# Attention preparation of a gated cross-attention and expert layer: split around the first scores, V times Wo formed turned

## The reference, cut to what matters

```
x1  = x + tanh(g_xattn) * attention(layernorm(x), ctx)
out = x1 + tanh(g_ffn)  * experts(layernorm(x1))

attention: q = xn Wq^T + bq;  k = ctx Wk^T + bk;  v = ctx Wv^T + bv
           softmax(q k^T / sqrt(512), masked) v Wo^T + bo
experts:   8 experts, each batch's expert takes its 512 best tokens; w1, exact gelu, w2
```

## Time and profile before

| | before |
|---|---|
| median of 3 runs (lowest, highest) | 1584.35 us (1581.07, 1585.58) |
| profiled execution, its own time | 1584.71 us |
| its span in the profile | 1583.0 us |
| mean granted TensorE clock | 0.981 |
| TensorE busy, matmuls and weight loads | 1504.1 us (95%), 1215.4 us (77%) |
| VectorE, ScalarE, GpSimd busy | 1015.0, 749.4, 573.8 us |
| DMA moved | 163.71 MB, mean 103 GB/s |

### The profile page before, as it was taken

One profiled execution on the slowest core, in us unless ns is written; L12 is line 12 of the kernel. 1 busy time (PEld: TensorE's weight loads), 2 busy tenths in 40 slices (PEclk: granted clock), 3 DMA queues, 4 the chain that ended last, 5 costly groups with the idle time before them and its releaser, 6 DMA issues.

```text
span 1583.0 us, 22317 instructions
## 1 busy us (share of the span) xinstructions
PE 1504.1 (95%) x7153; PEld 1215.4 (77%) x7153; DVE 1015.0 (64%) x1704; ACT 749.4 (47%) x1399; POOL 573.8 (36%) x541
## 2 busy tenths in 40 slices
PE   6887588999999999999999999999999999999996
PEld 6444367788788888888888888888888888888885
DVE  1378777556866766576766667576667665766542
ACT  1775133345544545454444454455445454554432
POOL 1265622453444234432444135404442344323311
PEclk9998699999999999999999999999999999999998
DMA  6075522462333442334323434243334423442133
GB/s 230 23 271 195 165 72 80 114 173 80 80 107 92 89 111 83 107 81 108 95 92 81 95 93 121 61 108 86 107 94 87 115 80 107 81 107 80 40 79 68
DMA packets 101479, 163.71 MB, mean 103 GB/s; under 512 B 7418, under 2 KB 45318, under 8 KB 101365
## 3 DMA queue, kind: packets, MB, share of 16 engines
q1 hardware_dynamic: 86965, 128.66, 26.1%
q0 software_dynamic: 14400, 33.56, 11.5%
HBM read 128.64 MB, written 33.55 MB: 102 GB/s over the span
## 4 chain that ended last, share of the span: by engine, by line
PE 85%; DVE 7%; ACT 3%; issue 2%; POOL 1%; DMA 1%; POOLq 0%; SPq 0%; ACTq 0%; DVEq 0%
PE bank L1289 41%; PE bank L1175 33%; PE bank L1149 3%; PE bank L1444 1%; PE bank L544 1%; PE bank L562 1%; DVE w2hl L1134 1%; PE bank L392 1%; DVE count L816 1%; DVE st L781 1%; DVE onehot L1330 1%; DVE atleast L863 1%; DMA ctx_raw<-in_ctx 0%; PE bank L414 0%; ACT xT L612 0%
## 5 line engine op out<-in xcount | busy, mean ns | idle before, releaser
L1289 PE MATMUL bank<-w2hl,hh 128*128 128x512 f32 x2048 | 637.6, 393 | 0.0
L1175 PE MATMUL bank<-xo,whl 128*128 128x512 f32 x2352 | 544.4, 390 | 3.8 <-DVE mix L1239 2.8
L1175 PEld LDWEIGHTS bank<-xo,whl 128*128 128x128 f32 x2352 | 442.1, 188 | 98.5 <-DVE mix L1239 3.7
L1289 PEld LDWEIGHTS bank<-w2hl,hh 128*128 128x128 f32 x2048 | 381.6, 188 | 76.2
L1289 PE MATMUL bank<-w2hl,hid_low 128*128 128x512 f32 x1024 | 399.6, 390 | 0.0
L1289 PEld LDWEIGHTS bank<-w2hl,hid_low 128*128 128x128 f32 x1024 | 192.9, 188 | 40.5
L1394 POOL DMA_INDIRECT layer_out<-y,slot_row x64 | 102.5, 1601 | 302.0 <-ACT y L1309 287.2
L1134 DVE TENSOR_TENSOR w2hl<-raw,w2hl 128x512 fp32r<-128x512 f32 x226 | 160.7, 732 | 54.3 <-ACT w2hl L1129 45.8
L1103 POOL TENSOR_TENSOR whl<-raw,whl 128x512 fp32r<-128x512 f32 x56 | 82.2, 1468 | 260.2 <-ACT whl L1069 260.2
L1129 ACT ACTIVATE w2hl<-raw 128x512 fp32r<-128x512 f32 x228 | 136.5, 624 | 59.9 <-DMA raw<-in_L_ffn_w 41.0
L1108 POOL TENSOR_TENSOR whl<-wsum,whl 128x512 fp32r<-128x512 f32 x56 | 75.0, 1340 | 183.4 <-ACT whl L1090 183.4
(11 more groups left out here) (221 smaller groups left out, 1808.3 us busy)
## 6 DMA issues: line engine op xcount, KB each, us to landing
raw<-in_L_ffn_w SPq DMA_DIRECT2D x228, 256.0 KB, 2.7
raw<-in_L_ffn_w SPq DMA_DIRECT2D x72, 512.0 KB, 4.9
x_s<-in_x SPq DMA_DIRECT2D x8, 1024.0 KB, 6.9
layer_out<-x SPq DMA_DIRECT2D x8, 1024.0 KB, 9.0
xn_rows<-xn SPq DMA_DIRECT2D x8, 1024.0 KB, 4.7
raw_k<-in_L_xattn_Wk SPq DMA_DIRECT2D x1, 1024.0 KB, 5.3
raw_q<-in_L_xattn_Wq SPq DMA_DIRECT2D x1, 1024.0 KB, 11.6
raw_v<-in_L_xattn_Wv SPq DMA_DIRECT2D x1, 1024.0 KB, 13.6
```

Of the source, the lines that this page charges most:

```text
L1175: last = pe.matmul(bk[:, :], whl[:, p % 2, part, 2 * w + k, :], xo[:, xpart, x, k, :], start=(not adds and k == 0 and part == HIGH and xpa ...
L1289: last = pe.matmul(Y_BANKS[c][:, :], high if hpart == HIGH else low[:, c * P:(c + 1) * P], w2hl[:, f % 4, part, :], start=(s == 0 and hpar ...
```

## The change

The list of steps is cut behind `mean`. TensorE, ScalarE and VectorE run the first part, then the attention's iteration 0 (the scores and exponentials of quad 0), and the second part at the head of iteration 1. The turns of Wv 1 and 2, which stood between `cb` and `mean`, are now in the second part; `turn_v` 0 stays in the first.

For the first three quads VectorE takes mean and variance of x by bn_stats and bn_aggr (`lead_stats_dve`), right after its copies of `turn_v` 0, `turn_o` 1 and `turn_o` 3; ScalarE's two passes begin with quad 3.

The product of V and Wo is formed turned: `voT` (two steps, Wo stationary, the 154 columns of both batches' values moving) comes first, VectorE adds bo as a column and multiplies by the gate in one operation, and `vo` is voT turned back. bo is loaded as four rows of 128 with the other biases instead of 77 copies of 512.

Wv, Wo and their turned forms lie in a place of their own (that of `xp` and `hid1`, used later), so that the attention's tiles can be written while they are in use.

```diff
+        outward = ExitStack()
+        with outward:
+            raw_v, raw_o, wvT, woT = (outward.enter_context(nc.sbuf_tensor(n, [P, KD, D], F32))
+                                      for n in ("raw_v", "raw_o", "wvT", "woT"))
         xp = overlay("xp", [P, B, 2, KD, CAP], F32R)
...
             with projections:
-                raw_k, raw_q, raw_v, raw_o, wkT, wvT, woT = (
-                    first(n, [P, KD, D], F32, projections)
-                    for n in ("raw_k", "raw_q", "raw_v", "raw_o", "wkT", "wvT", "woT"))
+                raw_k, raw_q, wkT = (first(n, [P, KD, D], F32, projections) for n in ("raw_k", "raw_q", "wkT"))
             xT = first("xT", [P, 2, KD, Q * P], F32)
...
         add("cb", 0, "act", ("kT", 1))
+        add("mean", 0, "dve", ("qk", 1))
+        SCORES_STEPS = len(steps)
         add("turn_v", 1, "dve")
         add("turn_v", 2, "act")
-        add("mean", 0, "dve", ("qk", 1))
         add("turn_v", 3, "act")
...
             add("turn_o", k, by_turns[k % 2])
+        for h in range(2):
+            add("voT", h, "dve", ("turn_o", KD - 1))
         for b in range(B):
-            add("vo", b, "dve", ("turn_o", KD - 1))
-        for b in range(B):
-            add("voT", b, "act", ("vo", b))
-        add("vg", 0, "dve", ("voT", B - 1))
+            add("vo", b, by_turns[b], ("voT", 1))
+        add("vg", 0, "dve")
         PREP_BANKS = (bank[0], bank[1], bank[5], bank[7])
-        BC = 3 * KD
+        BC = 4 * KD
...
-        def prep_pe(pe):
-            pe.wait_ge(consts, 1)
+        def prep_pe(pe, part):
+            if part == 0:
+                pe.wait_ge(consts, 1)
             for n, (name, i, _, after) in enumerate(steps):
+                if (n >= SCORES_STEPS) != (part == 1):
+                    continue
                 bk = PREP_BANKS[n % 4]
...
                                              start=(c == 0), stop=(c == KD - 1))
+                elif name == "voT":
+                    for h in range(2):
+                        for k in range(KD):
+                            c = 2 * i + h
+                            last = pe.matmul(bk[:, h * BJ:(h + 1) * BJ], woT[:, k, c * P:(c + 1) * P], vT[:, k, :],
+                                             start=(k == 0), stop=(k == KD - 1))
                 elif name == "vo":
-                    for c in range(KD):
-                        last = pe.matmul(bk[0:J, :], vT[:, c, i * J:(i + 1) * J], woT[:, c, :], start=(c == 0),
-                                         stop=(c == KD - 1))
-                elif name == "voT":
                     for k in range(KD):
-                        last = pe.transpose(bk[:, k * J:(k + 1) * J], vo[0:J, i, k * P:(k + 1) * P],
-                                            ident[0:J, 0:J])
+                        last = pe.transpose(bk[0:J, k * P:(k + 1) * P], voT[:, k, i, :], ident[:, :])
                 elif name == "vg":
...
-        def prep_out(eng, mine, is_act):
+        LEAD_AT = {("turn_v", 0): 0, ("turn_o", 1): 1, ("turn_o", 3): 2}
+        def lead_stats_dve(dve, own, q):
+            dve.wait_ge(x_in[q], 16)
+            wait(dve, lead_stats, q)
+            for i in range(Q):
+                own.mark(dve.bn_stats(st1[:, i, :], x_s[:, q, i, :]))
+            dve.wait_ge(dve_own, own.n)
+            for i in range(Q):
+                last = dve.bn_aggr(mv1[:, q, i, :], st1[:, i, :])
+                own.mark(last) if i < Q - 1 else last.then_inc(lead_stats, 1)
+        def prep_out(eng, mine, is_act, part, own=None):
...
                                              bk[:, 0:B * JE].unsqueeze(1).to_broadcast([P, KD, B * JE]), ALU.subtract)
+                elif name == "voT":
+                    eng.wait_ge(prep_act, 1)
+                    eng.wait_ge(gates_done, 1)
+                    for h in range(2):
+                        c = 2 * i + h
+                        last = eng.tensor_scalar(voT[:, c, :, :].rearrange("p b j -> p (b j)"),
+                                                 bk[:, h * BJ:(h + 1) * BJ], cols[:, 3 * KD + c:3 * KD + c + 1],
+                                                 gates[:, 0:1], ALU.add, ALU.mult)
                 elif name == "vo":
-                    eng.wait_ge(gates_done, 1)
                     eng.wait_ge(consts, 3)
-                    eng.tensor_tensor(vo[0:J, i, :], bk[0:J, :], bo_all[:, :], ALU.add).then_inc(vo_sum, 1)
-                    eng.wait_ge(vo_sum, i + 1)
-                    last = eng.tensor_scalar(vo[0:J, i, :], vo[0:J, i, :], gates[0:J, 0:1], None, ALU.mult)
-                elif name == "voT":
-                    last = copy(voT[:, :, i, :], bk[:, 0:KD * J].rearrange("p (k j) -> p k j", k=KD))
+                    last = copy(vo[0:J, i, :], bk[0:J, :])
                 elif name == "vg":
...
                 last.then_inc(mine, 1)
+                if not is_act and (name, i) in LEAD_AT:
+                    lead_stats_dve(eng, own, LEAD_AT[name, i])
...
                 q = it
+                if it == 1:
+                    prep_pe(pe, 1)
                 if q < NQ:
...
-                wait(act, squares_done, q)
+                wait(act, squares_done, q - LEAD)
                 for i in range(Q):
...
                 last.then_inc(x_summed, 1)
-                act.wait_ge(x_summed, q + 1)
+                act.wait_ge(x_summed, q - LEAD + 1)
                 act.activation(xmean[:, q % 2, :], xsum[:, q % 2, :], ACT.Copy, scale=-1.0 / D).then_inc(mean_ready, 1)
...
-                act.wait_ge(mean_ready, q + 1)
+                act.wait_ge(mean_ready, q - LEAD + 1)
                 wait(act, normed1, q - 1)
...
-            sums(0)
             for it in range(NQ + 1):
+                if it == 1:
+                    prep_out(act, prep_act, True, 1)
                 q = it
...
                 if q < NQ:
-                    squares(q)
+                    if q >= LEAD:
+                        squares(q)
                     act.wait_ge(turned, turn_at["s", q, 0] + 1)
...
                     act.activation(sT[:, q % 2, :], turn_bank(("s", q, 0))[0:JE, :], ACT.Copy).then_inc(turn_out, 1)
-                    if q + 1 < NQ:
+                    if LEAD <= q + 1 < NQ:
                         sums(q + 1)
...
                 s = q % 2
-                pool.wait_ge(squares_done, q + 1)
-                own.mark(pool.tensor_scalar(norm1[:, s, 0, :], xvar[:, s, :], 1.0 / D, EPS, ALU.mult, ALU.add))
+                if q < LEAD:
+                    pool.wait_ge(lead_stats, q + 1)
+                    own.mark(pool.tensor_scalar(norm1[:, s, 0, :], mv1[:, q, :, 1], EPS, None, ALU.add))
+                else:
+                    pool.wait_ge(squares_done, q - LEAD + 1)
+                    own.mark(pool.tensor_scalar(norm1[:, s, 0, :], xvar[:, s, :], 1.0 / D, EPS, ALU.mult, ALU.add))
                 pool.wait_ge(pool_own, own.n)
...
             for it in range(NQ + 1):
+                if it == 1:
+                    prep_out(dve, prep_dve, False, 1, own)
                 if it >= 2:
...
                      (bias_rows[2 * KD:3 * KD, :], bq.rearrange("(c p) -> c p", p=P)),
-                     (bo_all[:, :], bo.rearrange("(a d) -> a d", a=1).to_broadcast([J, D])),
+                     (bias_rows[3 * KD:4 * KD, :], bo.rearrange("(c p) -> c p", p=P)),
                      (gate_raw[:, :], gate_w)]
...
```

More of the change, by code:

```diff
@@ L63, in flamingo_layer @@
     NV = 5
+    LEAD = 3
     SCALE = float(D) ** -0.5
@@ L159, in flamingo_layer @@
             mean_m = first("mean_m", [P, P], F32)
-            bias_rows = first("bias_rows", [3 * KD, P], F32)
-            bo_all = first("bo_all", [J, D], F32)
+            bias_rows = first("bias_rows", [4 * KD, P], F32)
             gate_raw = first("gate_raw", [E, D], F32)
-            cols = first("cols", [P, 3 * KD + KD * E], F32)
+            cols = first("cols", [P, 4 * KD + KD * E], F32)
             ctx_raw = first("ctx_raw", [J, B, D], F32)
@@ L195, in flamingo_layer @@
             xvar = first("xvar", [P, 2, Q], F32)
+            st1 = first("st1", [P, Q, 6], F32)
+            mv1 = first("mv1", [P, LEAD, Q, 2], F32)
             st2 = first("st2", [P, Q, 6], F32)
@@ L232, in flamingo_layer @@
         gates_done = sem("gates_done")
-        vo_sum = sem("vo_sum")
+        lead_stats = sem("lead_stats")
         x_in = [sem(f"x_in{i}") for i in range(3)]
@@ L440, in prep_out @@
             for n, (name, i, by, _) in enumerate(steps):
-                if (by == "act") != is_act:
+                if (by == "act") != is_act or (n >= SCORES_STEPS) != (part == 1):
                     continue
@@ L1819, in _ @@
             act.activation(gates[:, :], gates_raw[:, :], ACT.Tanh).then_inc(gates_done, 1)
-            prep_out(act, prep_act, True)
+            prep_out(act, prep_act, True, 0)
             attention_act(act)
@@ L1846, in _ @@
             own = Tally(dve_own)
-            prep_out(dve, prep_dve, False)
+            prep_out(dve, prep_dve, False, 0, own)
```

(2 more changed lines are left out.)

## The result

The changed kernel takes 1576.50 us, the median of 7 runs (1572.15 to 1578.86). Beside it the kernel before took 1582.97 (7 runs, 1581.07 to 1585.58; the median of the 3 runs shown ahead of the prediction lay 1.4 above that). The ratio is 0.9958 with a 95% interval of 0.9943 to 0.9973, a gain of 6.5 us. In a later series on one chip it was 0.9952 (0.9937 to 0.9967).

The account below looks back on a forecast made before the run. TensorE, carrying 85% of the chain, was taken to bound the kernel, with preparation through quad 2's score product as one file. Gains of 5.3 and 0.7 less 1.3 for the clock gave 4.7 us: 1579.7 us, range 1576.6 to 1583.4.

Parts of the forecast that it names:

- the term of 1.3: TensorE's clock: half-clock stretches expected to cost 0.85 on vT and 0.45 in the second pause, 1.3 us together.
- both new pauses: TensorE without products at 36.75 to 42.5 and, with only small vg, 53.15 to 58.95; clock expected to fall in both.
- the other reading: Turns on TensorE do count as work for the clock; the sum would then be about 0.85 us better.
- The list of expected times: Step-by-step times from preparation to quad 2's score product at full clock, giving 5.3 us gained there.
- the new wait: TensorE stands until ScalarE's copies of Wv 2 and 3, behind quad 0's exponentials, are done at 42.45; about 2 to 3 us.
- quad 2's mark: Start of quad 2's score product, the yardstick: 75.92 before, 70.65 expected at full clock, near 71.2 in the changed profile.
- The removed load: Smaller bo load ahead of the context: context arrives 0 to 1.3 us earlier, 0.7 taken.
- What hides what: VectorE's statistics, 2.9 us a quad, and its copies lie beside other work and delay no product.
- (b): Rival: context moves 1.3 earlier and the first half-clock stretch misses vT; gain 6.6, 1578 us; chance 0.17.
- (c): Rival: half-clock stretches cost 3.2 on products and turns, context no earlier; gain 2, 1582.5 us; chance 0.18.
- (d): Rival: TensorE never regains 2.4 GHz between 41 and 59; 6.5 us slower, 1591 us; chance 0.05.
- (e): Rival: the split's copies and statistics are not hidden; gain under 1, 1584 us; inside (c)'s chance.

Follow-up runs that it names:

- e2: Changed kernel with the split undone, whole preparation ahead of quad 0 again; ratio to the kernel before 0.9978.
- e9: The kernel before, unchanged, profiled a second time; 1582.56 us, ratio 1.0003.
- e1: The kernel before with only the 77-row load of bo moved behind Wo; ratio to the kernel before 0.9994.
- e7: e6 with VectorE's statistics of quads 1 and 2 also moved, behind the copies of Wv 1 and the last preparation copy; 1571.65 us, ratio 0.9939.
- e10: The changed kernel, unchanged, run again on one chip with its variants; 1574.21 us, ratio to the kernel before 0.9952.
- e6: Changed kernel with four turns of Wv and Wo, and their copies, moved ahead of quad 0's exponentials; 1571.55 us, ratio to the kernel before 0.9939.
- e11: e2's unsplit form of the changed kernel again, on the same chip as e10; 1578.28 us, ratio to the kernel before 0.9975.
- e5: Changed kernel with TensorE waiting for quad 0's exponentials before the second half, so nothing runs in the pause; ratio to the kernel before 0.9983.
- e4: Changed kernel with the old straight product of V and Wo and the 77-row bo load (behind Wo) put back; ratio to the kernel before 0.9989.
- e3: Changed kernel with the statistics sums and squares of all quads back on ScalarE; ratio to the kernel before 0.9987.

## Why the prediction was right and wrong

- *The failed step* is the clock, the term of 1.3 lost. I expected both new pauses to fall; neither fell in either profile of the changed kernel. And I took the one fall of the first profile of the kernel before for that kernel's normal share, and read 0.5 for it. From start to start, as in e2, it cost 0.9 (quad 1's product starts 1.90 behind the last turn of x, quad 2's 12.26 later), and e9 and e1 lost 4 us more. The term should have been a gain, of 0.9 us against the first profile and 4.9 against the other two, instead of a loss. By the other reading that I gave, that turns count, the sum would have been 0.85 better, 5.55.
- *The base* was off too: 1584.35 was the median of 3 runs, and the 7 runs beside the changed kernel gave 1582.97, 31 runs in a later series 1582.29. The time was forecast 3.2 too high, of which 1.4 is the base and 1.8 the gain. Had either been right, the measured median would lie inside the range.
- *The list of expected times* held to 0.4 us. Starting 0.6 earlier, quad 0's product came at 32.65 (32.4 expected), the new wait ended at 42.19 (41.8 with the earlier start), the turned product took 4.44 (4.44), quad 2's mark was 70.34 (69.95). Against the kernel before at equal clock, 52.2 from kT to quad 2, the changed one has 48.18, so 4.0 are work and waits. Undone one at a time the old product costs 3.25, the statistics 1.15 (I had 1.0 for them in quad 0's start), the split 0.3 to 0.4; this adds up to 4.8, so the parts overlap. Of the 5.85 us between the two first profiles, then, 0.6 lie ahead of the end of kT, 4.0 are this work and these waits, 0.9 is the clock, and 0.3 lie behind quad 2's mark.
- *The removed load*: 0.7 taken, 0.63 between the two first profiles, but executions of one kernel differ by more (10.12 and 11.47 in the changed one).
- *What hides what*: VectorE's statistics delayed nothing beyond the 0.2 that e7 shows, as forecast. The copies behind the exponentials were named as the new wait. What the forecast never priced by itself is the split, from which this wait takes back nearly all.
- *The rivals*: (b), the gain of 6.6, came nearest, with a shift of the load of 0.6 for its 1.3, and no half-clock stretch at all where it had one that misses vT. The total fits it partly by luck, since the clock of the kernel before has its share. (c) and (d) did not occur. Of (e) the price did not come, but its doubt about the split was near the truth.

What stays open is the part of the gain behind quad 2's product. Execution time less that mark ran from 1505.1 to 1509.5 us over all fourteen profiles, and for the same kernel, the changed one, it was 1508.5 and 1505.4. Half-clock stretches near 250 and 420 us come and go between executions, and nothing here ties them to the change. They go with most of the spread: the nine profiles that have both lie at 1506.6 to 1509.5, and of the five with one or none four (e1, e10, e2, e7) lie at 1505.1 to 1505.6, e6 at 1507.1.

## What to carry to other kernels

When a stage is cut in two to cover a latency, look at which engine's queue the covered work's copies stand in: here the work was hidden on TensorE but copied by the engines that form the latency, and all but 0.3 to 0.4 us came back. An order of turns and copies that brings almost nothing at equal clock can still be worth microseconds, because work on TensorE in a pause, turns too, can help to keep its clock. And one profile of a kernel with pauses shows one draw of the clock: compare stretches at equal clock, and price the clock from several executions.

## What the runs showed of the hardware

The granted clock rose to the 2.4 GHz level on turns alone (13.3 us in e11, with turns without a break from 10.16), came back on turns alone (41.9 in e5), and stayed through 5.9 us in which only turns ran (the changed kernel, e10 and e4, not e3). It fell during 3.45 us of nothing (e5) and, in e9, after turns broken by idle times of 1.12 and 0.72 us, which the first profile of the same kernel had without a fall. With that one program it first rose at 20.4 and 15.4, and was down from 46.1 on for 10.2 us in one execution and not in the other.
